# Attention and mixture-of-experts layer on eight cores: weights as one DMA per slot, stores on SP's queue, six DMA lanes

## The reference

```python
x = x + attn(layernorm(x), W_qkv, b_qkv, W_out, b_out)   # 16 heads of 128, causal softmax
x = x + ffn(layernorm(x), ...)
# ffn, for each token:
logits = x @ gate_w.T                     # 8 experts, the best 2, softmax over the two
y  = sum over experts of comb[e] * ((silu(x @ Wg[e]) * (x @ Wu[e])) @ Wd[e])   # 2048 -> 512 -> 2048
y += (silu(x @ sWg) * (x @ sWu)) @ sWd    # shared expert, 2048 -> 1024 -> 2048
```

## Time and profile before

| | |
|---|---|
| median of five runs | 6345.82 us (6319.12 to 6690.93) |
| the profiled execution | 6336.33 us, span 6334.7 us on its slowest core (core 2) |
| spans of the eight cores | 6276.0 to 6334.7 us |
| TensorE busy | 4759.9 us, 75% of the span |
| VectorE, ScalarE, GpSimd busy | 33%, 24%, 13% |
| mean granted TensorE clock, core 2 | 0.831 |
| chain that ended last, by engine | PE 54%, DVE 13%, POOL 10%, ACT 7%, DMA 7%, issue 7% |
| DMA traffic by queue | GpSimd's 176.32 MB, SP's 138.72 MB, ScalarE's 67.13 MB |

### The profile page before, as it was taken

How to read it: one execution, slowest core, us unless ns; L and a number is a source line. 1 busy time by engine, 2 the same in 40 slices (tenths; PEclk the granted TensorE clock), 3 DMA queues, 4 the chain that set the end, 5 groups by cost and what they waited for, 6 DMA issues and landing times.

```text
span 6334.7 us, 81039 instructions; the slowest of 8 cores (6276.0 to 6334.7 us)
## 1 busy us (share of the span) xinstructions
PE 4759.9 (75%) x23321; PEld 2180.4 (34%) x23680; DVE 2104.2 (33%) x4448; ACT 1525.1 (24%) x2532; POOL 825.8 (13%) x1541
## 2 busy tenths in 40 slices
PE   5755788889667776777767759688888928888984
PEld 2332344444333333333333324333333413333331
DVE  2130111100455544555455514322222233322214
ACT  2220122221444444444444410100000111000010
POOL 8049200000000000000000000121212011212120
PEclk9878898899776767677677779799999969999997
DMA  9257312211100000000000044453434252334243
GB/s 136 79 122 81 70 60 69 69 46 39 54 34 18 18 18 34 18 18 18 28 18 11 1 117 173 103 72 48 70 51 70 50 168 45 56 64 69 52 67 113
DMA packets 294181, 387.38 MB, mean 61 GB/s; under 512 B 133249, under 2 KB 256385, under 8 KB 274817
## 3 DMA queue, kind: packets, MB, share of 16 engines
q0 software_dynamic: 221328, 176.32, 18.7%
q1 hardware_dynamic: 21746, 138.72, 6.4%
q10 hardware_dynamic: 50688, 67.13, 2.9%
HBM read 457.61 MB, written 83.89 MB: 85 GB/s over the span
## 4 chain that ended last, share of the span: by engine, by line
PE 54%; DVE 13%; POOL 10%; ACT 7%; DMA 7%; issue 7%; DVEq 1%; ACTq 0%; SPq 0%; POOLq 0%
DVE cmax L474 6%; PE psC L784 6%; PE psA L377 6%; PE psB L377 6%; ACT pt L483 5%; PE psA L816 4%; POOL wkv L366 4%; PE psD L790 4%; POOL slot L696 3%; PE psC L552 3%; PE psA L468 3%; PE psD L552 3%; PE psB L790 3%; PE psB L468 3%; DMA slot<-wu 2%
## 5 line engine op out<-in xcount | busy, mean ns | idle before, releaser
L468 PE MATMUL psA<-qf,kf 128*128 128x512 bf16 (+3 forms) x1216 | 524.1, 453 | 206.2 <-DVE cmax L474 84.5
L468 PE MATMUL psB<-qf,kf 128*128 128x512 bf16 (+3 forms) x1280 | 517.6, 435 | 147.1 <-DVE cmax L474 62.0
L816 PE MATMUL psA<-slot,tdf 128*128 128x512 bf16 x2032 | 480.3, 378 | 41.4 <-ACT tdf L231 19.8
L784 PE MATMUL psC<-slot,hnf 128*128 128x512 bf16 x1934 | 461.6, 392 | 64.7 <-DMA slot<-wg 57.5
L377 PE MATMUL psA<-xnf_r,wkv 128*128 128x512 bf16 x2002 | 469.8, 391 | 46.9 <-DMA wkv<-wqkv_t 43.0
L377 PE MATMUL psB<-xnf_r,wkv 128*128 128x512 bf16 x2007 | 462.9, 386 | 47.2 <-DMA wkv<-wqkv_t 44.9
L483 ACT ACTIVATE pt<-psA,biasap 128x512 bf16<-128x512 f32 (+3 forms) x640 | 402.3, 629 | 389.1 <-DVE psA L480 215.5
L474 DVE TENSOR_REDUCE cmax<-psA 128x1 f32<-128x512 f32 (+1 forms) x640 | 407.5, 637 | 139.0 <-PE psT L226 88.1
L483 ACT ACTIVATE pt<-psB,biasap 128x512 bf16<-128x512 f32 (+3 forms) x640 | 395.5, 618 | 110.4 <-DVE psB L480 60.7
L254 DVE TENSOR_SCALAR xn<-xt,sm 128x2048 bf16<-128x2048 f32 x52 | 70.3, 1353 | 1041.5 <-ACT sm L251 1041.5
L822 DVE SCALAR_TENSOR_TENSOR y_sb<-psA,y_sb 128x512 f32<-128x512 f32 x512 | 354.2, 692 | 153.5 <-PE psA L816 112.8
(11 more groups left out here) (118 smaller groups left out, 5187.2 us busy)
## 6 DMA issues: line engine op xcount, KB each, us to landing
xt<-x_own SPq DMA_DIRECT2D x36, 1024.0 KB, 7.4
xt<-x_seq SPq DMA_DIRECT2D x32, 1024.0 KB, 5.0
slot<-wg POOLq DMA_DIRECT2D x256, 128.0 KB, 5.6
slot<-wu POOLq DMA_DIRECT2D x256, 128.0 KB, 9.3
slot<-wd POOLq DMA_DIRECT2D x64, 512.0 KB, 16.5
wkv<-wqkv_t POOLq DMA_DIRECT2D x512, 32.0 KB, 4.8
kf_s<-kst ACTq DMA_DIRECT2D x128, 128.0 KB, 1.9
vf_s<-kst ACTq DMA_DIRECT2D x128, 128.0 KB, 1.9
```

Of the source, the lines that this page charges most:

```text
L468: em.emit("t", lambda E, kt=kt, g=g, hb=hb, jmin=jmin, N=N, stb=stb: E.matmul(stb[:, 0:N], kf_sb[hb][:, kt * 128:(kt + 1) * 128], qf_sb[hb ...
L784: (lambda E, i=i, t=t, jg=jg: E.matmul(g_ps[:], hnf[:, i * TPP * 128 + t * 128: i * TPP * 128 + (t + 1) * 128], slot[jg][:, i * 512:(i + 1 ...
L816: (lambda E, mc=mc, oc=oc, kb=kb, jd=jd, yj=yj: E.matmul(y_ps[yj], tdf_7[kb][:, mc * 128:(mc + 1) * 128], slot[jd][:, mc * 2048 + oc * 512 ...
```

## The change

It has three parts. The number of lanes of a queue goes from 8 to 6. The stores of Q, K, V, `h` and `hn` are issued from SP's queue instead of ScalarE's, at the same places of the program order; so on SP they stand between the loads of `xt`. And the weights of experts and shared expert are laid out on the host so that each partition's 8192 f32 values of a slot are contiguous (32 KB), and one DMA loads a slot. Which bytes land where in a slot is unchanged.

```diff
-    def __init__(self, nc, stack, lanes=8):
+    def __init__(self, nc, stack, lanes=6):
...
-    wg = d("wg", [NEXP, 16, 128, M], F32, "ExternalInput")
+    wg = d("wg", [NEXP, 128, 8192], F32, "ExternalInput")
...
-                em.dma("s", lambda E, o=o, n=n, sj=sj: E.dma_start(
+                em.dma("y", lambda E, o=o, n=n, sj=sj: E.dma_start(
                     out=qf_s[o][:, n * 512:(n + 1) * 512], in_=qst[sj][:]),
...
-                    em.dma("s", lambda E, o=o, n=n, sj=sj: E.dma_start(
+                    em.dma("y", lambda E, o=o, n=n, sj=sj: E.dma_start(
                         out=kf_s[o - 16][:, n * 512:(n + 1) * 512], in_=kst[sj][:]),
...
-                    em.dma("s", lambda E, o=o, n=n, sj=sj: E.dma_start(
+                    em.dma("y", lambda E, o=o, n=n, sj=sj: E.dma_start(
                         out=vf_s[o - 32][:, n * 512:(n + 1) * 512], in_=kst[sj][:]),
...
-            em.dma("s", lambda E, qt=qt, k=k: E.dma_start(out=h_s[qt], in_=ht_6[k][:]),
+            em.dma("y", lambda E, qt=qt, k=k: E.dma_start(out=h_s[qt], in_=ht_6[k][:]),
...
-            em.dma("s", lambda E, qt=qt, k=k: E.dma_start(out=hn_s[qt], in_=hn_6[k][:]),
+            em.dma("y", lambda E, qt=qt, k=k: E.dma_start(out=hn_s[qt], in_=hn_6[k][:]),
...
         def wg_loader(src, e):
-            return [(lambda E, S_, i=i, src=src, e=e: E.dma_start(
-                out=S_[:, i * 512:(i + 1) * 512], in_=src[e, i])) for i in range(16)]
+            return [(lambda E, S_, src=src, e=e: E.dma_start(out=S_[:], in_=src[e]))]
 
         def wd_loader(e):
-            return [(lambda E, S_, mc=mc, e=e: E.dma_start(
-                out=S_[:, mc * 2048:(mc + 1) * 2048], in_=wd[e, mc])) for mc in range(4)]
+            return [(lambda E, S_, e=e: E.dma_start(out=S_[:], in_=wd[e]))]
...
-    wg = c(np.asarray(Wg, np.float32).reshape(8, 16, 128, 512))
+    wg = c(np.asarray(Wg, np.float32).reshape(8, 16, 128, 512)
+           .transpose(0, 2, 1, 3).reshape(8, 128, 8192))
```

More of the change, by code:

```diff
@@ L154, in build_nc @@
     gate_wt = d("gate_wt", [16, 128, NEXP], F32, "ExternalInput")
-    wg = d("wg", [NEXP, 16, 128, M], F32, "ExternalInput")
[L156 to L160, removed]
+    wg = d("wg", [NEXP, 128, 8192], F32, "ExternalInput")
+    wu = d("wu", [NEXP, 128, 8192], F32, "ExternalInput")
+    wd = d("wd", [NEXP, 128, 8192], F32, "ExternalInput")
+    swg = d("swg", [2, 128, 8192], F32, "ExternalInput")
+    swu = d("swu", [2, 128, 8192], F32, "ExternalInput")
+    swd = d("swd", [2, 128, 8192], F32, "ExternalInput")
     mask_in = d("mask", [128, 256], F32, "ExternalInput")
@@ L695, in wg_loader @@
         def wg_loader(src, e):
-            return [(lambda E, S_, i=i, src=src, e=e: E.dma_start(
-                out=S_[:, i * 512:(i + 1) * 512], in_=src[e, i])) for i in range(16)]
+            return [(lambda E, S_, src=src, e=e: E.dma_start(out=S_[:], in_=src[e]))]
         def wd_loader(e):
-            return [(lambda E, S_, mc=mc, e=e: E.dma_start(
-                out=S_[:, mc * 2048:(mc + 1) * 2048], in_=wd[e, mc])) for mc in range(4)]
+            return [(lambda E, S_, e=e: E.dma_start(out=S_[:], in_=wd[e]))]
         def sw_loader(src, half):
-            return [(lambda E, S_, i=i, src=src, half=half: E.dma_start(
-                out=S_[:, i * 512:(i + 1) * 512], in_=src[i][:, half * 512:(half + 1) * 512]))
-                for i in range(16)]
+            return [(lambda E, S_, src=src, half=half: E.dma_start(out=S_[:], in_=src[half]))]
         def swd_loader(half):
-            return [(lambda E, S_, mc=mc, half=half: E.dma_start(
-                out=S_[:, mc * 2048:(mc + 1) * 2048], in_=swd[half * 4 + mc])) for mc in range(4)]
+            return [(lambda E, S_, half=half: E.dma_start(out=S_[:], in_=swd[half]))]
         y_ps = [psA[:, 0:512], psA[:, 512:1024]]
@@ L926, in host_prep @@
     gate_wt = c(np.asarray(gate_w, np.float32).T.reshape(16, 128, 8))
-    wg = c(np.asarray(Wg, np.float32).reshape(8, 16, 128, 512))
[L928 to L932, removed]
+    wg = c(np.asarray(Wg, np.float32).reshape(8, 16, 128, 512)
+           .transpose(0, 2, 1, 3).reshape(8, 128, 8192))
+    wu = c(np.asarray(Wu, np.float32).reshape(8, 16, 128, 512)
+           .transpose(0, 2, 1, 3).reshape(8, 128, 8192))
+    wd = c(np.asarray(Wd, np.float32).reshape(8, 4, 128, 2048)
+           .transpose(0, 2, 1, 3).reshape(8, 128, 8192))
+    _swg_r = np.asarray(sWg, np.float32).reshape(16, 128, 1024).transpose(1, 0, 2)
+    swg = c(np.stack([_swg_r[:, :, hh * 512:(hh + 1) * 512].reshape(128, 8192)
+                      for hh in (0, 1)]))
+    _swu_r = np.asarray(sWu, np.float32).reshape(16, 128, 1024).transpose(1, 0, 2)
+    swu = c(np.stack([_swu_r[:, :, hh * 512:(hh + 1) * 512].reshape(128, 8192)
+                      for hh in (0, 1)]))
+    swd = c(np.asarray(sWd, np.float32).reshape(2, 4, 128, 2048)
+            .transpose(0, 2, 1, 3).reshape(2, 128, 8192))
     ii = np.arange(128)[:, None]
```

## The result

The changed kernel takes 1.0107 times the time before, with a 95% interval of 1.0061 to 1.0152: about 68 us more. On the median before of all ten runs, 6339.88 us, that is 6408; the prediction was 6371, with 6325 to 6430 as its range. In most executions of the changed kernel four or all of the cores had a lower granted clock, which is why the ratio leaves these out, its plain median of 6703.71 says nothing, and its trace is read on core 4, which was not among them (clock 0.829, span 6391.4). Core 4 before had 6323.2, so the two spans differ by 68.2 as well.

What follows compares the result with a forecast made beforehand. It took TensorE's idle waits, for LayerNorm at block changes and for expert weights, as the bound. 6336.3 + 77 (block changes) + 3 (output projection) - 45 (weights) = 6371 us, range 6325 to 6430.

Steps and rivals of the forecast that it cites:

- three signs of being wrong: Written rates reach 218, `hnt` lands after 11 us, or `xt` still lands ahead of the last ACTIVATE.
- Part 1: Q and K/V stages: stores on SP end the prefetch at nine block changes, 8.5 us each, 77 us lost; bounds 75 to 100.
- 0.42 until the load is issued: Block change: SP's delay from the store to the next load's issue, 0.33 us and a gap of 0.09.
- 4.9 until it has landed: Block change: time in us from the issue of the `xt` load to its landing.
- Part 2: Output projection: with `h` and `hn` stores on SP a tile keeps 15.5 us; +3 us, from -3 to +20.
- Part 3: Six lanes for eight: only `wout` loads fill the window and the queue doesn't run dry; worth nothing.
- Part 4: Expert weights, one DMA per slot: wu lands earlier, 2.5 us on average at 18 places, 45 us gained.
- two slots, 4.19 MB as written, at the same steady rate: Expert weights: transfers take 24.8 us in pass 1, 21.0 in pass 2; start and end add 2.5.
- no number of issues lifts either rate by more than 6%: Expert weights: read rates of 338 and 400 GB/s stand 6% under 358 and 425; at most 1.4 us a place.
- Rival A: Expert weights gain nothing: first stretch stays slow or long rows cost GpSimd 2.5 us; time 6416, chance 0.20.
- Rival C: Expert weights: many small DMAs hold the rate down; gain 6.2 us a place, 112 in all, time 6298, chance 0.15.
- Rival B: Pass starts: long rows starve `hnt` loads, landing after 11 us or more; 35 us lost, time 6406, chance 0.12.

Runs made afterwards that it cites:

- e1: Kernel before with only the stores of Q, K, V, `h` and `hn` moved to SP's queue, old weights, eight lanes: ratio 1.0135, +86 us.
- e7: As e1, but the first two loads of the next block are emitted ahead of this block's stores: ratio 1.0006 to the kernel before.
- e8: Kernel before with only the stores of `h` and `hn` moved to SP's queue: ratio 0.9998.
- e5: Kernel before with one DMA per wg or wu expert slot from the old layout, rows still 2 KB: single run 6327.76 us, no interval.
- e6: Kernel before with the new weight layout, each expert slot in four DMAs of 8 KB rows, shared expert's slots in one: ratio 0.9944.
- e4: As e2, but each pass's first expert comes in 16 DMAs of 2 KB rows (wg, wu) and 4 of 8 KB (wd): ratio 0.9916 to kernel before.
- e9: As e2, but each pass's first wg load waits until the last `hnt` tile is transposed: ratio 0.9884 to the kernel before, 73 us less.
- e2: Kernel before with only the new weight layout and one DMA per slot; stores and lanes unchanged: ratio 1.0032 (0.9984 to 1.0080).

## Why the prediction came out half a size short

The direction and the range held; the forecast was 35 us above the kernel before, and 68 were measured. Part of that is luck: the loss at the block changes was forecast 15 us too small and the gain in the experts 16 us too small, and the two cancel. What is left of the error is the loss at the pass starts, which the sum put at nothing. Of the three signs of being wrong that it named, one came true in full (`hnt` landed after 27.9 us where the mark was 11), and one nearly (written rates of 216, where the mark was 218). By its own steps:

- **Part 1, the stores of Q, K and V: right, a term under-sized.** 8.5 a place and 77 were forecast, 9.9 at the place shown and 92 / 9 = 10.2 on average were measured. Two parts of the sum were small. "0.42 until the load is issued" was 0.74 from the end of the eviction where 0.08 + 0.42 were worked out. And "4.9 until it has landed" was the landing of a load that leaves alone; here two leave together, and the first has landed after 872.46 - 866.39 = 6.1. The 4.38 of the LayerNorm held to the hundredth. The 92 lie nearer to the upper bound of 100 than to the 77. e1 shows the size by itself, e7 that the order on SP is all of it.
- **Part 2, `h` and `hn`: right.** 15.4 us a tile, `xt` landing in 6.1, and a stage shorter by 4 on core 4 (by 2 on average over cores 4 to 7) rather than longer by 3. e8 alone shows no difference.
- **Part 3, lanes: nearly right.** 0.2 to 0.5% was found where nothing was forecast. At the 16 loads of `wout`, where the argument looked, it was right that nothing changes; where the loss is stays open.
- **Part 4, the gain: right in sign, under-sized, with the wrong cause.** 45 was forecast and 61 measured on core 4, 53 on average over cores 4 to 7. The step that failed is "two slots, 4.19 MB as written, at the same steady rate". In pass 2, where the rates are steady, 201 became 216; e5 and e6 show that 200 is what rows of 2 KB give, and not what the memory and the engines give. A share of 1.24 did not mean that the engines moved all they could, as longer rows moved more bytes at 1.02. The other half of the term was off the other way: at 216 GB/s two slots take 19.4 us, and 23.0 were measured (core 4, average of pass 2), so that start and end came to 3.6 and not 2.5. In pass 1 the 169 of core 2 was no property of the program: core 0 wrote 195 to 201 at its changes of expert, and needed 25.1 us on average where core 2 needed 29.9. That the second pass is faster because both cores of a pair load in the first, as the forecast has it in its rivals A and C, no run shows. The view of DMA packets shows how the rows changed, first core 4 before from 4455 to 4475, then after from 4460 to 4478:

```profile
DMA packets 3332, 3.05 MB, mean 153 GB/s; under 512 B 366, under 2 KB 3331, under 8 KB 3331
```

```profile
DMA packets 240, 3.67 MB, mean 204 GB/s; under 512 B 16, under 2 KB 16, under 8 KB 16
```

- So "no number of issues lifts either rate by more than 6%" was true of the number of issues (e5) and false of this change, which also lengthened the rows. The Trainium skill (HBM Reference, Specifications (TRN2)) has about 358 GB/s for each of two cores that stream and about 425 for one alone. The steady 216 as written are 432 as read in f32, just above the second figure; the 165 of a first change in pass 1 are 330, under the first. Whether the other core of the pair was loading at either moment the traces can't tell, so no run here confirms or refutes the two figures.
- **What an issue costs: right.** 0.53 us was taken for an issue with rows of 32 KB, and 0.53 is what the trace has.
- **Rival A** fell, with the gain itself. **Rival C** had half of the truth: the steady rates came to 216 of the 218 that it had as a mark, and the gain to 61 of its 112; but its cause, many small DMAs, is worth 6 of 15 GB/s and no time (e5), and long rows (e6) are in its place.
- **Rival B was dismissed and was right.** It had a chance of 0.12, 35 us and the time 6406; 37 us and 6408 were measured. The 35 us are its own; that the time fits as well is the luck of the two errors that cancel. The step that failed is the argument against it, "none lands later than 9.3, though wd's rows of 8 KB cross them too". wd's rows are a third of the weights and a quarter as long; from them nothing followed for all three slots with 32 KB. Its arithmetic, a turn of 1.3 us for each of eight rows and so "11 us or more" for a load, meets the spacing of 12 to 16 us. The Trainium skill (DMA: Bandwidth & Descriptors, Queues, rings and completion order) has an engine change queues only between packets of several descriptors. The trace agrees so far as the loads behind long rows waited up to 27.9 us; row by row or packet by packet no run here tells apart. e4 and e9 show the cause by taking the long rows away from `hnt`.

The forecast's steps with the measured sizes give 92 - 4 + 37 - 61 = 64, and attention's 4.6 makes 68; that last term is scatter between cores, as cores 4 to 7 have 2063.3 before and 2063.6 after on average. The parts tried one by one (e1, e2, lanes) have ratios that add up to 1.018 to 1.020, against 1.0107 for the whole; with the 0.999 of e2's two shorter runs it is 1.014 to 1.016. The intervals (up to 1.0152 for the whole) leave room for both, and no run shows an interaction of the parts.

## What to carry to other kernels

When a store moves to a queue that also carries loads, look at what stands behind it in program order: the queue waits with the store for its data, and a prefetch behind it is a prefetch no more. The cure is to emit the load ahead of the stores, not to change the queue. Judge a weight load by the length of its DRAM rows rather than by the number of DMAs, and once it is fast, keep it away from short-row loads that something waits for: 8 KB rows, short rows where the two meet, or one after the other.

## What the runs showed of the hardware that was not expected

- DMAs of GpSimd that cast f32 to bf16 wrote in steady stretches of pass 2 201 GB/s with DRAM rows of 2 KB in 16 DMAs, 207 with the same rows in one DMA (share 1.24 in both), 214 with rows of 8 KB (share 1.06) and 216 with rows of 32 KB (share 1.02).
- Loads of 0.5 MB with rows of 4 KB: the slowest on a core landed in 4.7 to 5.4 us with no expert weights beside them (e9), 7.8 to 9.6 beside rows of 2 KB (before), 10.1 to 13.1 beside rows of 8 KB (e6) and 22.2 to 29.6 beside rows of 32 KB (after, e2).
- An issue on GpSimd took 0.53 us for 128 rows of 32 KB, as for 128 rows of 2 or 8 KB, and 1.17 for 2048 pieces of 2 KB: 16 times the pieces, 2.2 times the time.
- Two 1 MB loads issued together on SP, behind a store of 128 KB: the first was there after 6.1 us, where one alone took 4.9 in the kernel before.
